# A bound on every gathered index in a graph network kernel

## The chip, the core and the metric

The kernel runs on one core of one Trainium2 chip. The metric is the time of one execution on the device, in microseconds (us). The median of three runs of the kernel before is 1931.74 us, with 1929.56 us as the lowest and 1933.11 us as the highest.

The engines are named as in the profile: PE is the matrix engine (PEld its weight loads), DVE, ACT and POOL are the vector, scalar and GpSimd engines, and SP is the engine that here only issues transfers. POOL is the one engine that issues an indirect DMA: a transfer that takes a list of row numbers from SBUF and fetches those rows of a table in HBM.

## The reference

There are 2,500 nodes with 256 features each, and 82,500 edges, sorted by their destination. Every edge has a source, a destination, a type from 0 to 7 and a weight. The first block is a relational graph convolution of two layers with a residual and a layer norm; the second is a network of three mean-aggregation layers with a residual and a layer norm.

```python
def _L0_gnn_ref(feat, norm, basis, coeff, bias, src, dst, etype):
    h = feat
    for l in range(2):
        W = jnp.einsum('rb,bio->rio', coeff[l], basis[l])
        all_h = jnp.einsum('ni,rio->rno', h, W)
        msg = all_h[etype, src] * norm
        agg = jax.ops.segment_sum(msg, dst, num_segments=2500)
        h = agg + bias[l]
        if l < 1:
            h = jax.nn.relu(h)
    return h

def _L1_gnn_ref(x, W_in, b_in, W_agg, W_self, b_hid, W_out, b_out, edge_index):
    dst, src = edge_index
    h = x @ W_in + b_in
    deg = jnp.maximum(jax.ops.segment_sum(ones, dst, 2500), 1.0)[:, None]
    for l in range(3):
        agg = jax.ops.segment_sum(h[src], dst, 2500) / deg
        h = jax.nn.relu(agg @ W_agg[l] + h @ W_self[l] + b_hid[l])
    return h @ W_out + b_out

x = _layernorm(x + _L0_gnn_ref(x, edge_weight1, ..., src, dst, edge_type_8))
x = _layernorm(x + _L1_gnn_ref(x, ..., stack([src, dst])))
```

## The kernel before

**Tiles of edges.** The edges are cut into T = 645 tiles of 128; the last tile holds 68. Each of the two layers of the first block (l = 0 and l = 1) goes through all tiles, so there are 1,290 tile visits, numbered n = l * 645 + t. In each visit the kernel needs the source row of each of the tile's edges: 128 rows of 1 KB, from the input `x` in layer 0 and from the DRAM table `H1`, the output of layer 0, in layer 1.

**Who fetches the rows.** In 14 of the visits (7 in each layer, ROW_TILES) SP fetches the rows one by one with plain transfers into `GS` (L1136). In the other 1,276 visits POOL fetches them, with one indirect DMA for a tile, issued by `rows_of` at L352 into one of NG = 16 slots of `G`. The row numbers are a column of `si`, or of `siF` for the first 15 tiles of layer 1. `G` is a part of the large tile `RY`, so the profile names such a gather `RY<-in_x,si`, `RY<-H,RX` or `RY<-H,si`.

**What orders the gathers.** `pool_setup` issues the first 16, and `pool_fast` the other 1,260 in order. Before each it waits on `s_sum` until PE has used the rows of the gather 16 places earlier, which frees the slot. Before layer 1 it waits for `H1` to be stored. After the last gather POOL converts eight blocks for the second part and does some of its output work.

**What uses the rows.** For every three tiles PE runs 12 matmuls at L1037 (`pe_sums_of`): the gathered rows are the weights, and a selection matrix that DVE makes from type, destination and edge weight (L631) is the moving operand. PE waits on `s_land[slot]` for the rows. DVE adds the sum to a window of accumulators (L623), and PE multiplies each finished window with the weights of the eight types (L885). Between these, in an order written out by hand, PE counts edges into an adjacency matrix (L867, L868) and, in layer 1, runs the first aggregation of the second block on windows that are done (L935). The second and third aggregation follow (L1281, L1247, L1291) and then the output (L1353); no gather is left by then.

A second program for inputs that don't fit this plan (`pool_general`) stands in the kernel too. It has indirect DMAs of its own, and isn't executed here.

Of the kernel before, what the change touches and what calls it, by code (L numbers as in the profile page):

```python
# [56 lines left out]
def edge_rows(t):  # L57
    return 128 if t < T - 1 else LASTP
# [110 lines left out]
def program(nc, x, ramp, ramp_col, src_rows, srcT, dstT, etT, wT, large, small, basis, coeff, bias, W_in, b_in, W_agg, W_self,  # L169
# [11 lines left out]
    with ExitStack() as ctx:  # L181
# [167 lines left out]
        def rows_of(e, n, table, index):  # L349
            t, slot = n % T, PLACE[n] % NG  # L350
            k = edge_rows(t)
            e.indirect_dma_start(G[0:k, slot, :], None, table, bass.IndirectOffsetOnAxis(ap=index[0:k, t:t + 1], axis=0)).then_inc(  # L352
                s_land[slot], 16)

        def pool_setup(e):
            e.wait_ge(s_src0, 16)
            for t in range(FIRST):
                rows_of(e, t, x, si)
# [75 lines left out]
        def pool_fast(e):  # L434
            e.wait_ge(s_src, 16)
            for p in range(FIRST, len(POOLED)):
                n = POOLED[p]
                e.wait_ge(s_sum, POOLED[p - NG] + 1)
                if n == T:
                    e.wait_ge(s_fixi, 4)  # L440
                    e.wait_ge(s_zrow, 32)
                    e.wait_ge(s_h1, 16 * (NW - 1))
                if n == T + FIX:
                    e.wait_ge(s_h1, 16 * NW)
                rows_of(e, n, x if n < T else H1, siF if T <= n < T + FIX else si)
            e.wait_ge(s_sum, 2 * T)
            e.wait_ge(s_dpe, NC * JB)
            e.wait_ge(s_ad, 16 * NA)
            for n in range(NR):
                e.wait_ge(s_ah[0], 16)  # L450
                e.tensor_copy(Ar[0:PB, n, :], Ah[0][:, n, :]).then_inc(s_arP, 1)
            for j in range(JB - 1):
                pool_bias(e, j)
            pool_norm(e, 16)
            pool_bias(e, JB - 1)
            pool_norm(e, 17)
            pool_norm(e, 18)
# [1470 lines left out]
```

## Time and profile before

| | |
|---|---|
| median of 3 runs | 1931.74 us (1929.56 to 1933.11) |
| span of the profiled execution, first to last instruction | 1935.5 us |
| PE busy | 1657.1 us (86%) |
| POOL busy | 1243.6 us (64%) |
| DVE busy | 1168.4 us (60%) |
| ACT busy | 487.5 us (25%) |
| mean busy share of the DMA engines, indirect gathers alone | 30.4% |
| mean granted TensorE clock | 0.963 of full speed |

The profile gives the profiled execution's time only as its span; it is 3.8 us (0.2%) above the median of the timed runs. An engine's busy time is the sum of its instructions. A line like `L352 POOL DMA_INDIRECT RY<-in_x,si x638` is one group of instructions: the line in the kernel, the engine, the operation, what it writes and reads, and how many there are. "idle before" is the time in which that engine stood still just before such an instruction, and the name after the arrow is what ended it; "issue" stands where nothing that the profile shows ended it. The share of busy time is an average over stages with different limits, so the stages are read one by one.

### The profile page before, as it was taken

The page shows a single profiled execution, that of the slowest core. Times are in us where ns is not written, and L with a number is a line of the kernel's source. Part 1 is how long each engine was busy: PE and PEld are TensorE (multiplying, and loading weights), DVE is VectorE, ACT ScalarE, POOL GpSimd, SP SyncE. Part 2 cuts the span into 40 slices and gives each one's busy share as a digit, 9 for nine tenths or more (in the row PEclk, how much of TensorE's full clock was granted, in tenths as well). Part 3 has the DMA queues.
Part 4 walks back from the last instruction along what each step waited for, and adds up shares of the span by engine and source line. Part 5 has one row for each costly group of instructions (what it writes and reads, how often), then busy time and mean ns, then how long its engine had stood idle before and what let it go on. Part 6 is the DMA issues. An engine that isn't in the chain of part 4 may idle for free.

```text
span 1935.5 us, 36034 instructions
## 1 busy us (share of the span) xinstructions
PE 1657.1 (86%) x9643; PEld 1378.2 (71%) x9643; DVE 1168.4 (60%) x4021; ACT 487.5 (25%) x1018; POOL 1243.6 (64%) x1311
## 2 busy tenths in 40 slices
PE   5787787887777778888899898888989999999997
PEld 3676666676566667676777787777777887777775
DVE  7978856656565656566777676775555563322344
ACT  2002111111211111122322222232455113433322
POOL 6777777777777777777777777777777773000011
PEclk9889999889999999999999999999999899999999
DMA  7344444444444444444444444445555442310011
GB/s 266 107 112 119 116 117 116 121 116 117 119 118 115 121 116 116 113 137 124 132 125 133 131 127 127 131 132 140 163 167 152 118 136 60 85 44 1 12 42 44
DMA packets 147633, 222.02 MB, mean 115 GB/s; under 512 B 81009, under 2 KB 103298, under 8 KB 147428
## 3 DMA queue, kind: packets, MB, share of 16 engines
q0 software_dynamic: 61344, 167.21, 30.4%
q1 hardware_dynamic: 49988, 38.78, 7.0%
q10 hardware_dynamic: 36096, 13.70, 2.6%
q8 instruction: 80, 1.31, 0.3%
q14 instruction: 125, 1.02, 0.2%
HBM read 202.31 MB, written 17.27 MB: 113 GB/s over the span
## 4 chain that ended last, share of the span: by engine, by line
PE 53%; DMA 31%; POOL 7%; issue 4%; DVE 3%; ACT 1%; DVEq 0%; ACTq 0%; POOLq 0%
PE bank L1037 21%; DMA RY<-in_x,si 19%; DMA RY<-H,si 12%; PE bank L1281 9%; PE bank L885 9%; POOL RY L352 7%; PE bank L935 3%; PE bank L1247 2%; PE bank L1291 2%; PE bank L868 1%; PE bank L1353 1%; PE bank L1002 1%; PE bank L852 1%; PE bank L950 1%; PE bank L908 1%
## 5 line engine op out<-in xcount | busy, mean ns | idle before, releaser
L1037 PE MATMUL bank<-RY 128*128 128x128 f32 x5104 | 768.9, 291 | 221.3 <-DMA RY<-in_x,si 146.8
L1037 PEld LDWEIGHTS bank<-RY 128*128 128x128 f32 x5104 | 678.9, 199 | 324.4 <-DMA RY<-in_x,si 187.7
L352 POOL DMA_INDIRECT RY<-in_x,si x638 | 611.2, 958 | 198.1 <-issue 136.9
L352 POOL DMA_INDIRECT RY<-H,si x623 | 595.0, 955 | 190.1 <-issue 138.4
L631 DVE TENSOR_SCALAR RY<-iot,c,wgt 128x128 f32<-128x128 f32 x1290 | 455.7, 358 | 389.3 <-PE bank L1037 388.2
L720 ACT CAST RY<-bank 128x320 uint8<-128x320 f32 x215 | 91.6, 426 | 684.2 <-PE bank L868 672.9
L509 DVE TENSOR_SCALAR RY<-iotN,bcol 128x320 bf16<-128x320 f16 x645 | 209.1, 324 | 0.0
L1281 PE MATMUL bank<-Ar,hs 125*128 125x500 f32 x800 | 203.9, 405 | 0.0
L623 DVE TENSOR_TENSOR RY<-RY,bank 128x256 f32 x430 | 178.4, 415 | 24.5 <-issue 13.0
L885 PE MATMUL bank<-RX,RY 128*128 128x256 f32 x704 | 189.1, 397 | 3.0 <-issue 1.8
L1342 POOL TENSOR_TENSOR x1b<-x1b,bo 125x256 f32<-125x256 f32 x20 | 14.8, 741 | 272.7 <-DMA x1b<-X 272.7
L885 PE MATMUL bank<-RY 128*128 128x256 f32 x704 | 184.3, 388 | 3.6 <-DVE RY L623 3.6
L868 PE MATMUL bank<-RY 128*128 128x320 bf16 x645 | 175.3, 310 | 0.5 <-DVE RY L509 0.5
L508 DVE TENSOR_SCALAR RY<-iotN,c 128x128 bf16<-128x128 f16 x645 | 175.2, 272 | 0.0
L1281 PEld LDWEIGHTS bank<-Ar,hs 125*128 125x128 f32 x800 | 150.6, 188 | 33.2 <-issue 4.6
L885 PEld LDWEIGHTS bank<-RY 128*128 128x128 f32 x704 | 129.5, 195 | 22.9 <-DVE RY L623 5.9
L885 PEld LDWEIGHTS bank<-RX,RY 128*128 128x128 f32 x704 | 130.8, 201 | 18.7 <-issue 2.0
L708 ACT COPY RY<-zero 128x576 f32<-128x576 f32 x176 | 109.5, 667 | 27.4 <-ACT RY L720 23.1
L935 PE MATMUL bank<-ArP,hsP 128*128 128x500 f32 x380 | 115.8, 425 | 0.4 <-DVE sagg L556 0.4
L777 ACT COPY RY<-bank 128x256 f32<-128x256 f32 x44 | 16.4, 373 | 314.6 <-PE bank L890 271.8
L556 DVE TENSOR_TENSOR sagg<-bank,sagg 128x500 f32<-128x500 f32 x90 | 60.6, 673 | 51.2 <-PE bank L935 51.1
L868 PEld LDWEIGHTS bank<-RY 128*128 128x128 bf16 x645 | 65.6, 102 | 27.1 <-issue 3.6
(148 smaller groups left out, 1311.3 us busy)
## 6 DMA issues: line engine op xcount, KB each, us to landing
ei<-in_x SPq DMA_DIRECT2D x896, 1.0 KB
ei<-H SPq DMA_DIRECT2D x896, 1.0 KB
RY<-in_x,si POOLq DMA_INDIRECT x638
RY<-H,si POOLq DMA_INDIRECT x623
Ad<-RY ACTq DMA_DIRECT2D x215, 40.0 KB
A<-Ad SPq DMA_DIRECT2D x22, 312.5 KB, 3.3
D<-Ad SPq DMA_DIRECT2D x20, 305.2 KB
RX<-in_basis ACTq DMA_DIRECT2D x2, 2048.0 KB, 21.7
```

Of the source, the lines that this page charges most:

```text
L352: e.indirect_dma_start(G[0:k, slot, :], None, table, bass.IndirectOffsetOnAxis(ap=index[0:k, t:t + 1], axis=0)).then_inc(s_land[slot], 16)
L508: e.tensor_scalar(Mr[:, u % NSL, :], iotN[:, 0:128], c1[:, u:u + 1], None, ALU.is_equal)
L509: e.tensor_scalar(Nr[:, u % NSL, :], iotN[:, :], bcol[:, u:u + 1], None, ALU.is_equal).then_inc(s_hot, 1)
L623: e.tensor_tensor(o, o, bank[2 + wg % 3][:, 0:256].rearrange("p (q c) -> p q c", c=16), ALU.add).then_inc(s_za, 1)
L631: e.tensor_scalar(S[:, v % NSS, :], iot[:, :], c2[:, u:u + 1], wgt[:, u:u + 1], ALU.is_equal, ALU.mult).then_inc(s_sel, 1)
L708: e.copy(o, zero[:, 0:1].to_broadcast([128, 4 * ZC])).then_inc(s_clear, 1)
L720: e.copy(Aw8[:, w % 4, :], bank[6 + w % 2][:, 0:NB]).then_inc(s_aw8, 1)
L868: e.matmul(b[:, 0:NB], Mr[0:k, a % NSL, :], Nr[0:k, a % NSL, :], start=(a == 0), stop=(i == TA - 1)).then_inc(s_cnt, 1)
L885: mm = e.matmul(bank[0][:, 0:256], ZA[:, s, q, 0:128], W[:, c, r * 256:(r + 1) * 256], start=(q == 0), stop=(g == 0 and q == 15))
L935: mm = e.matmul(unit_bank(q)[:, 0:CH], hsP[:, g % NP, part, mo * 128:(mo + 1) * 128], ArP[:, n % NV, :], start=(i + part == 0), stop=(i == ...
L1037: mm = e.matmul(bank[2 + wg % 3][:, c * 128:(c + 1) * 128], rows, S[0:k, n % NSS, :], start=(i == 0 and not ahead), stop=(i == TA - 1))
L1281: mm = e.matmul(bank[bs[mo]][:, 0:CH], hs[0:PB, j, q, mo * 128:(mo + 1) * 128], Ar[0:PB, n % NR, :], start=(j == 0 and q == 0), stop=(j == ...
```

## The change

The call of `indirect_dma_start` in `rows_of` gets two more arguments. `bounds_check` names the highest row number that counts as valid, here the table's last row: 2499 for `x`, and 2500 for `H1`, which has one row more. `oob_is_err=False` says that an index above the bound is no error: its row isn't copied, and nothing is reported. Without the two arguments, as before, no bound is named and the error mode is at its default, true. All indices in this input lie within the bound, so the same rows are moved. All 1,276 gathers are issued by this one call; the ones of `pool_general` go through another one and stay as they are.

```diff
         def rows_of(e, n, table, index):
             t, slot = n % T, PLACE[n] % NG
             k = edge_rows(t)
-            e.indirect_dma_start(G[0:k, slot, :], None, table, bass.IndirectOffsetOnAxis(ap=index[0:k, t:t + 1], axis=0)).then_inc(
+            e.indirect_dma_start(G[0:k, slot, :], None, table, bass.IndirectOffsetOnAxis(ap=index[0:k, t:t + 1], axis=0), bounds_check=table.shape[0] - 1, oob_is_err=False).then_inc(
                 s_land[slot], 16)
```

## Rows read from the trace of the kernel before

**Rows 1.** The page: busy time, and busy tenths in 40 slices.

```profile
PE 1657.1 (86%) x9643; PEld 1378.2 (71%) x9643; DVE 1168.4 (60%) x4021; ACT 487.5 (25%) x1018; POOL 1243.6 (64%) x1311
...
POOL 6777777777777777777777777777777773000011
```

**Rows 2.** The page: the chain of work that ended last, by engine.

```profile
PE 53%; DMA 31%; POOL 7%; issue 4%; DVE 3%; ACT 1%; DVEq 0%; ACTq 0%; POOLq 0%
```

**Rows 3.** Line L352 alone: durations in ns (min/median/max), first and last start.

```profile
L352 POOL DMA_INDIRECT RY<-in_x,si x638: 942/947/1682, 4.4 to 808.5; - x160
L352 POOL DMA_INDIRECT RY<-H,si x623: 942/947/1219, 830.3 to 1613.9; - x156
L352 POOL DMA_INDIRECT RY<-H,RX x15: 942/947/1009, 811.3 to 829.0; - x15
```

**Rows 4.** Timeline of POOL in layer 0: start us, duration us, instruction, idle before.

```profile
299.56 0.96 POOL L352 DMA_INDIRECT RY<-in_x,si  x1 [0.30 <-issue]
300.82 0.95 POOL L352 DMA_INDIRECT RY<-in_x,si  x1 [0.30 <-issue]
302.07 0.95 POOL L352 DMA_INDIRECT RY<-in_x,si  x1 [0.30 <-issue]
303.33 0.95 POOL L352 DMA_INDIRECT RY<-in_x,si  x1 [0.30 <-PE bank L1037]
```

**Rows 5.** Groups by line, PE's and POOL's: busy us, mean ns, idle before, releasers.

```profile
L1037 PE MATMUL bank<-RY 128*128 128x128 f32 x5104 | 768.9, 291 | 221.3 <-DMA RY<-in_x,si 146.8 <-DMA RY<-H,si 59.8 <-issue 7.0
...
L352 POOL DMA_INDIRECT RY<-in_x,si x638 | 611.2, 958 | 198.1 <-issue 136.9 <-PE bank L1037 57.3 <-DMA si<-in_srcT 4.0
L352 POOL DMA_INDIRECT RY<-H,si x623 | 595.0, 955 | 190.1 <-issue 138.4 <-PE bank L1037 51.6
```

**Rows 6.** Busy time by stage: window and length, then PE, PEld, DVE, ACT, POOL.

```profile
400.00:600.00 200.00, 156.34 (x972) 128.80 (x971) 119.45 (x473) 33.58 (x71) 151.53 (x160) 0.97 0.42 117
...
1090.00:1350.00 260.00, 229.58 (x1456) 196.66 (x1455) 178.63 (x661) 74.46 (x161) 197.19 (x207) 0.97 0.47 131
1350.00:1500.00 150.00, 138.24 (x881) 114.20 (x880) 77.25 (x221) 79.80 (x161) 113.73 (x120) 1.00 0.58 160
1500.00:1614.00 114.00, 110.40 (x645) 94.33 (x644) 67.97 (x182) 24.71 (x53) 86.15 (x92) 0.94 0.45 126
```

**Rows 7.** Timeline of POOL where layer 0 ends, its last tile (68 rows) at 808.54.

```profile
807.29 0.95 POOL L352 DMA_INDIRECT RY<-in_x,si  x1 [0.30 <-PE bank L1037]
808.54 1.22 POOL L352 DMA_INDIRECT RY<-in_x,si  x1 [0.30 <-issue]
811.34 0.96 POOL L352 DMA_INDIRECT RY<-H,RX  x1 [1.57 <-DMA H<-RY]
```

**Rows 8.** Timeline of POOL where layer 1 ends, its last tile at 1613.93.

```profile
1612.68 0.95 POOL L352 DMA_INDIRECT RY<-H,si  x1 [0.30 <-issue]
1613.93 1.10 POOL L352 DMA_INDIRECT RY<-H,si  x1 [0.30 <-PE bank L1037]
1624.47 4.45 POOL L451 CAST Ar<-AhG 125x500 fp32r<-125x500 uint8 x8 [9.43 <-PE bank L1037]
```

**Rows 9.** Timeline of POOL at the start of the program.

```profile
0.25 0.10 POOL L1921 MEMSET const-float32-0.0<- 128x1 f32 x1 [0.25 <-issue]
0.28 0.10 POOL L1921 MEMSET const-float32-1.0<- 128x1 f32 x1
0.31 0.10 POOL L1921 MEMSET const-bfloat16-1.0<- 128x1 bf16 x1
...
4.43 1.16 POOL L352 DMA_INDIRECT RY<-in_x,si  x1 [4.00 <-DMA si<-in_srcT]
```

**Rows 10.** Timeline of PE where layer 1 ends: its last work on gathered rows.

```profile
1620.20 1.50 PE L1037 MATMUL bank<-RY 128*128 128x128 f32 x12
1621.46 1.60 PE L974 MATMUL bank<-ArP,hsP 128*128 128x500 f32 x6
1622.90 1.50 PE L1037 MATMUL bank<-RY 128*128 128x128 f32 x12
```

## The prediction

> **What bounds the kernel now.** I read the page first. PE is busy 86% of the span and POOL only 64%, but POOL's slices stand at an unbroken 7, from the second slice to the 32nd, and fall to nearly 0 after that [rows 1]. A share that never moves for 1,600 us is either an engine waiting in a steady rhythm or one that never waits at all. The chain of work that ended last puts 31% of the span on landing DMAs and 7% on POOL, beside 53% on PE [rows 2]. So a good part of the end is set by gathers, and the question is what paces them: the slot that has to come free, the transfer, or POOL's own time for issuing one.
>
> The timeline of POOL answers it. A gather starts every 1.25 us: 0.95 us busy and 0.30 us idle [rows 4]. The idle time is 0.30 us when "issue" ended it, and 0.30 us when a wait for PE's sums is named too, so that wait had long been met. The whole groups say the same: 388 us of idle before 1,276 gathers is 0.30 us for each [rows 5]. The gathers run from 4.43 us to 1613.93 + 1.10 = 1615.03 us [rows 8, 9], and 1610.6 us / 1,276 is 1.262 us. POOL is therefore saturated from the first gather to the last; the missing tenths in the page are a gap that belongs to each gather. The times are also strikingly even: 942 ns at least, 947 ns as the median, in all three groups and with whatever row numbers [rows 3].
>
> PE on its side waits for gathered rows: 146.8 us in layer 0 and 59.8 us in layer 1, in its matmul groups [rows 5]. In the stages, PE is busy 156 of 200 us in the middle of layer 0 and 230 of 260 us in the middle of layer 1, but 248.6 of 264 us from 1350 us to the end of the gathers [rows 6]. So POOL sets the pace up to about 1350 us (638 gathers of layer 0 and some 430 of layer 1), and for the last 208 or so both run at about the same pace, with PE a little behind. Between the last gather's end at 1615.0 us and PE's last matmuls on gathered rows at 1622.9 us lie 7.9 us [rows 8, 10]; a gather of 3 to 4 us in flight leaves some 4 us of slack at that point.
>
> **What the change does, part by part.** No instruction is added to PE, DVE, ACT or SP, no wait is added or removed, no buffer or order moves, and the same rows in the same transfers are fetched, since no index lies above the bound. What can change is what POOL does for each of 1,276 gathers. Anything it does is on the path: a microsecond on POOL before 1350 us is a microsecond at the end, since nothing there covers it. Behind a late gather stand the next gathers on POOL's own queue; 3 tiles' sums on PE wait for it, then DVE's add to the window, and the whole rest of the layer.
>
> The trace has no gather with a bound, so each part is priced from both sides by the nearest rows.
>
> (a) Handing the bound to the gather. At least nothing: it can travel in the instruction, or be set once for each of the two tables. At most one more small instruction on POOL for each gather. The four memsets at the start begin 0.03 us apart [rows 9], and I take that as the price of one more small instruction in POOL's stream. The ends are 0 and 0.03 us, and I take the middle, 0.015 us. By the Trainium skill ("Advanced Engine Details and Errata", Engine Queue Depths) GpSimd has a queue of 8 entries, so its sequencer may run ahead of the work and such an instruction would be hidden: by that rule this part is 0 instead of 1,276 x 0.015 = 19 us. That the gap of 0.30 us doesn't grow when a wait is named [rows 4] agrees with it, though it doesn't prove it.
>
> (b) Comparing 128 row numbers with the bound, and being ready to leave rows out. It falls into the busy part, 947 ns for 128 rows, or 7.4 ns a row if all of it went by rows. At least nothing: the comparison can be there already, against a bound that never bites; the nearest row is the distance from the minimum to the median, 5 ns [rows 3]. At most what an unusual gather costs here: the two of 68 rows take 1.22 and 1.10 us [rows 7, 8] against 0.947 us for 128 rows. Fewer rows take longer, so POOL has a quick way for the full tile and another for the rest, and the other is up to 0.27 us longer. Between 0.005 and 0.27 us, a factor of 54 apart, I take the geometric middle, 0.037 us; it is about 4% of the busy part, which is what one more test among the steps that make a row's transfer would be.
>
> (c) Dropping the error mode. It removes work only if some is done now, when no bound is named that an index could break. I take 0, and keep a gain as a rival.
>
> The sum is 0.015 + 0.037 = 0.052 us a gather, and 1,276 x 0.052 = 66 us. Off it goes the slack at the end of layer 1, about 4 us, because the last 208 gathers come 208 x 0.052 = 11 us later to a PE that is that much behind. PE's later stages, from 1623 us on, hang on no gather. So the span goes from 1935.5 to about 1997.5 us, +62 us, and the median of the runs, which stands 3.8 us lower, from 1931.7 to 1993.7 us; I forecast 1993 us. With the two upper ends together it is 1,276 x 0.30 = 383 us, 2,310 us; with both lower ends nothing.
>
> **The rivals.**
>
> *Nothing changes* (chance 0.34). The comparison is always made, or hides inside the 947 ns, and the bound costs no instruction. For it: the duration doesn't depend on the index values, which is how it would look if the work were done over many rows at once, where one comparison more is a few ns. Under 3 ns a gather it is 1,276 x 0.003 = 4 us, 0.2% of the time, and that is about what a measurement of this kernel can tell from no change. Time: 1928 to 1936 us.
>
> *Faster* (0.17). Place: the end of each gather at L352, where an error would be reported. If the default mode costs a check there, the new mode drops it. A price in the size of the one small instruction, 0.03 us, would reach the end wherever PE waits for rows: (638 + 430) x 0.03 = 32 us, 1900 us; the last 208 gain nothing, since PE has no idle time left to give. It decides as soon as what it saves exceeds (a) and (b) together, 0.052 us if those are real and 0.003 us if they are not. Its limit is PE's 206.6 us of waiting for gathers [rows 5], 1725 us. Against it: nothing in the trace shows such a check, and no bound is named before that could be broken.
>
> *The full tile loses its quick way* (0.05). If the bound sends every gather through a way that treats row by row, the 68-row gather prices it: 1.10 us / 68 x 128 = 2.07 us, 1.12 us more than 0.947, and 1,276 x 1.12 = 1,430 us gives 3,360 us. It decides if any step has to branch for each row. The Trainium skill ("GPSIMD Engine Reference", section 3.1) says that data-dependent branching costs about 12 cycles an element, at 1.2 GHz (its section 1): an estimate by that page is 128 x 12 / 1.2 = 1,280 ns a gather, 1,633 us in all, 3,565 us. The page speaks of elements of a kernel's loop, and a rarely taken branch need not cost that; against the rule stands that now a whole row costs at most 7.4 ns, 9 cycles of that clock, with every step of it.
>
> **How the numbers follow.** The forecast's mechanism, POOL longer by 0.003 to 0.30 us a gather, gets 0.44; with the lost quick way slower holds 0.49, nothing 0.34, faster 0.17. The likeliest one's own range goes from 0.01 us a gather (+12 us, 1944 us) to 0.235 us (+300 us, 2230 us). The range for the time has to take in "nothing" as well, and the smaller gains: from 1905 us, which is a gain of 0.025 us on 1,068 gathers, to 2230 us. Outside are the larger gains (about 0.10), the lost quick way (0.05) and the last part of the mechanism (0.04).
>
> **What the profile of the changed kernel would show.** The first place is line L352 alone: its median against 947 ns is (b), and its idle before against 0.30 us is (a). The period of POOL times 1,276 must give the end of the last gather, now 1615 us. If POOL is longer, PE's idle time behind `DMA RY<-in_x,si` grows by nearly 638 times the difference, and behind `DMA RY<-H,si` by less than that; PE's busy time stays. If the two 68-row gathers no longer stand out from the others, the way has changed. The stretch after the last gather should stay as long as now, about 320 us, in every case.
>
> **What would make it wrong.** A comparison that is already made or that costs single ns; a default error mode that has a price; or a price per row that is far over 4% of the present time. The direction rests on POOL having no cover; the size rests on (b), which no row of the trace shows.

## The result, and the profile after

The changed kernel takes 2000.77 us as the median of 4 runs (1998.78 to 2003.65), and the kernel before 1931.83 us in runs beside it (4 runs, 1929.56 to 1933.11). The ratio is 1.0354, with a 95% interval of 1.0341 to 1.0367: 69 us slower. The forecast was 1993 us and 62 us slower.

Line L352 alone, in the kernel after (durations in ns as minimum/median/maximum, then first and last start in us), beside [rows 3]:

```profile
L352 POOLq MOVE  x1276: 29/29/38, 4.0 to 1668.0; - x183
L352 POOL DMA_INDIRECT RY<-in_x,si x638: 994/998/1842, 4.9 to 844.2; - x160
L352 POOL DMA_INDIRECT RY<-H,si x623: 994/998/1273, 865.9 to 1682.8; - x156
L352 POOL DMA_INDIRECT RY<-H,RX x15: 994/999/1223, 845.9 to 864.6; - x15
```

Two things are new. Each gather's median went from 947 to 998 ns, nearly alike in all three groups, and the minimum rose as much (from 942 to 994 ns). So every gather pays it, and it is no wait. And there is one MOVE of 29 ns for each gather on POOLq, POOL's own instruction queue; that it puts the bound into a register is borne out by the kernel with one register below. The timeline of POOL in layer 0 shows that it isn't seen between the gathers, whose idle time is 0.30 us as in [rows 4]:

```profile
299.62 1.02 POOL L352 DMA_INDIRECT RY<-in_x,si  x1 [0.30 <-issue]
300.94 1.00 POOL L352 DMA_INDIRECT RY<-in_x,si  x1 [0.30 <-issue]
302.24 0.99 POOL L352 DMA_INDIRECT RY<-in_x,si  x1 [0.30 <-issue]
303.54 1.00 POOL L352 DMA_INDIRECT RY<-in_x,si  x1 [0.30 <-issue]
```

The groups by line (busy us, mean ns, idle before and what ended it), beside [rows 5]:

```profile
L1037 PE MATMUL bank<-RY 128*128 128x128 f32 x5104 | 787.9, 294 | 266.8 <-DMA RY<-in_x,si 166.6 <-DMA RY<-H,si 83.4 <-issue 8.3
...
L352 POOL DMA_INDIRECT RY<-in_x,si x638 | 646.1, 1013 | 198.8 <-issue 142.7 <-PE bank L1037 51.6 <-DMA si<-in_srcT 4.5
L352 POOL DMA_INDIRECT RY<-H,si x623 | 628.2, 1008 | 190.1 <-issue 143.7 <-PE bank L1037 46.4
```

The page's sums, beside [rows 1]:

```profile
PE 1677.5 (84%) x9643; PEld 1389.0 (70%) x9643; DVE 1164.9 (58%) x4021; ACT 487.5 (24%) x1018; POOL 1313.1 (66%) x1311
```

POOL is busy 1313.1 - 1243.6 = 69.5 us longer, and the kernel takes 69 us longer. The idle time before the gathers is the same to a microsecond (198.8 and 190.1 us, against 198.1 and 190.1 us). PE's share of the change is split: it waits 43 us longer for gathered rows (250.0 against 206.6 us), and is busy 20 us longer, at a mean granted clock of 0.958 against 0.963. The last gather of each layer on POOL's timeline, beside [rows 7] and [rows 8]:

```profile
844.17 1.17 POOL L352 DMA_INDIRECT RY<-in_x,si  x1 [0.30 <-issue]
845.88 1.02 POOL L352 DMA_INDIRECT RY<-H,RX  x1 [0.55 <-issue]
...
1682.77 1.16 POOL L352 DMA_INDIRECT RY<-H,si  x1 [0.31 <-issue]
1687.60 4.43 POOL L451 CAST Ar<-AhG 125x500 fp32r<-125x500 uint8 x8 [3.66 <-PE bank L1037]
```

The last one ends at 1683.9 us, 68.9 us after that of the kernel before. Both layers have their part: layer 1's first gather, which waits for `H1` to be stored, starts at 845.88 in place of 811.34 us, 34.5 us later, and the rest is added after it. From the last gather to the end of the span it is 314.5 us, 6 us less than before (320.5 us). PE's timeline shows what became of the slack at the end of layer 1:

```profile
1685.06 0.73 PE L1037 MATMUL bank<-RY 128*128 128x128 f32 x4
1686.36 1.16 PE L1037 MATMUL bank<-RY 68*128 68x128 f32 x8 [0.57 <-DMA RY<-H,si]
```

PE now waits 0.57 us for the last gather itself, and starts on its rows 2.4 us after POOL is done with it. In the kernel before PE's last matmuls ran without a wait, 7.9 us after it [rows 10]. How much of the 6 us is the change's is taken up with the slack, further down.

### The profile page after: what moved, and what is told of

Same layout as the page of the kernel before. It is cut to its first block, busy times and chain, and to the rows that moved or that the text cites. A ratio compares the mean times of both kernels' runs of the same rounds, so it can differ in the third digit from the quotient of the medians.

```text
span 1998.4 us, 37310 instructions
## 1 busy us (share of the span) xinstructions
PE 1677.5 (84%) x9643; PEld 1389.0 (70%) x9643; DVE 1164.9 (58%) x4021; ACT 487.5 (24%) x1018; POOL 1313.1 (66%) x1311
## 3 DMA queue, kind: packets, MB, share of 16 engines
q0 software_dynamic: 61344, 167.21, 29.5%
## 4 chain that ended last, share of the span: by engine, by line
PE 46%; DMA 32%; issue 10%; POOL 9%; DVE 2%; ACT 1%; POOLq 0%; DVEq 0%; ACTq 0%
PE bank L1037 19%; DMA RY<-in_x,si 18%; DMA RY<-H,si 13%; PE bank L1281 9%; POOL RY L352 9%; PE bank L885 6%; PE bank L935 2%; PE bank L1247 2%; PE bank L1291 2%; PE bank L868 1%; PE bank L1353 1%; PE bank L852 1%; PE bank L908 1%; PE bank L1002 1%; PE bank L950 1%
## 5 line engine op out<-in xcount | busy, mean ns | idle before, releaser
L1037 PE MATMUL bank<-RY 128*128 128x128 f32 x5104 | 787.9, 294 | 266.8 <-DMA RY<-in_x,si 166.6
L1037 PEld LDWEIGHTS bank<-RY 128*128 128x128 f32 x5104 | 688.8, 201 | 379.8 <-DMA RY<-in_x,si 215.4
L352 POOL DMA_INDIRECT RY<-in_x,si x638 | 646.1, 1013 | 198.8 <-issue 142.7
L352 POOL DMA_INDIRECT RY<-H,si x623 | 628.2, 1008 | 190.1 <-issue 143.7
L631 DVE TENSOR_SCALAR RY<-iot,c,wgt 128x128 f32<-128x128 f32 x1290 | 460.9, 362 | 445.0 <-PE bank L1037 441.3
L509 DVE TENSOR_SCALAR RY<-iotN,bcol 128x320 bf16<-128x320 f16 x645 | 198.3, 307 | 0.0
L885 PE MATMUL bank<-RX,RY 128*128 128x256 f32 x704 | 184.9, 391 | 2.8 <-issue 1.9
L868 PE MATMUL bank<-RY 128*128 128x320 bf16 x645 | 178.1, 314 | 0.2
L935 PE MATMUL bank<-ArP,hsP 128*128 128x500 f32 x380 | 121.1, 441 | 0.4 <-DVE sagg L556 0.4
L868 PEld LDWEIGHTS bank<-RY 128*128 128x128 bf16 x645 | 66.0, 102 | 27.2 <-issue 3.1
```

Of the source, the lines that this page charges most:

```text
L509: e.tensor_scalar(Nr[:, u % NSL, :], iotN[:, :], bcol[:, u:u + 1], None, ALU.is_equal).then_inc(s_hot, 1)
L631: e.tensor_scalar(S[:, v % NSS, :], iot[:, :], c2[:, u:u + 1], wgt[:, u:u + 1], ALU.is_equal, ALU.mult).then_inc(s_sel, 1)
L868: e.matmul(b[:, 0:NB], Mr[0:k, a % NSL, :], Nr[0:k, a % NSL, :], start=(a == 0), stop=(i == TA - 1)).then_inc(s_cnt, 1)
L885: mm = e.matmul(bank[0][:, 0:256], ZA[:, s, q, 0:128], W[:, c, r * 256:(r + 1) * 256], start=(q == 0), stop=(g == 0 and q == 15))
L935: mm = e.matmul(unit_bank(q)[:, 0:CH], hsP[:, g % NP, part, mo * 128:(mo + 1) * 128], ArP[:, n % NV, :], start=(i + part == 0), stop=(i == ...
L1037: mm = e.matmul(bank[2 + wg % 3][:, c * 128:(c + 1) * 128], rows, S[0:k, n % NSS, :], start=(i == 0 and not ahead), stop=(i == TA - 1))
```

## Experiments

Every ratio below is against the kernel before on the same chip. The first four ran where the kernel before takes 1933 us, the next four where it takes 2275 us, and the last four where it takes 2296 us. What that means for them stands with the fifth.

### Which part of the change costs

**The bound alone, an index over it being an error.**

```diff
-            e.indirect_dma_start(..., axis=0)).then_inc(
+            e.indirect_dma_start(..., axis=0), bounds_check=table.shape[0] - 1).then_inc(
```

> The bound alone, with the error mode left at its default. Theory (the test of the row numbers costs): the median gather stays at 998 ns, idle before it at 0.30 us, the time within 0.3% of the changed kernel, about 2000 us. Rival (leaving rows out silently is what costs, by a way that must be ready to drop a row): with an index over the bound as an error the gather goes back towards 947 ns and the time to about 1932 us.

Measured: 2019.48 us, ratio 1.0445 (1.0428 to 1.0463), which is 86 us slower than before and some 18 us slower than the changed kernel. Line L352 alone:

```profile
L352 POOLq MOVE  x1276: 29/29/35, 4.1 to 1688.1; - x183
L352 POOL DMA_INDIRECT RY<-in_x,si x638: 1007/1012/1552, 5.0 to 854.4; - x160
L352 POOL DMA_INDIRECT RY<-H,si x623: 1007/1012/1229, 877.3 to 1701.3; - x156
```

The bound is what costs, and neither theory had the rest right: with the bound named, treating an index over it as an error costs another 14 ns (1012 against 998), and dropping the error mode saves that.

**The mode alone.**

```diff
-            e.indirect_dma_start(..., axis=0)).then_inc(
+            e.indirect_dma_start(..., axis=0), oob_is_err=False).then_inc(
```

> oob_is_err=False alone, no bound named. Theory: no index is tested, the median gather stays at 947 ns, no register instruction appears on POOL's queue, the time is within 0.2% of 1932 us. Rival (the mode costs): 998 ns and about 2000 us. Second rival (the default mode costs something, which the changed kernel's bound hides): under 947 ns, and faster by up to 1,276 times the difference, 13 us for each 10 ns.

Measured: 1931.83 us, ratio 0.9994 (0.9985 to 1.0004). Line L352 alone:

```profile
L352 POOL DMA_INDIRECT RY<-in_x,si x638: 942/946/1682, 4.2 to 807.8; - x160
L352 POOL DMA_INDIRECT RY<-H,si x623: 942/946/1212, 829.5 to 1611.5; - x156
```

Nothing changes. So the default mode costs nothing as long as no bound is named, and the "faster" rival has nothing to gain.

**The register set once for each table.**

```diff
+        def set_limit(e, rows):
+            if not limit:
+                limit.append(e.alloc_register("limit"))
+            e.reg_mov(limit[0], rows - 1)
...
-            e.indirect_dma_start(..., axis=0)).then_inc(
+            e.indirect_dma_start(..., axis=0), bounds_check=limit[0], oob_is_err=False).then_inc(
```

`set_limit` is called ahead of the first gather and again ahead of layer 1.

> The changed kernel with the bound in a register that is set once for each table, in place of one MOVE of 29 ns for each gather. Theory (the MOVE is hidden, the gather's own 51 ns are the cost): gather 998 ns, period 1.30 us, about 2000 us, no gain. Rival (the MOVE is part of the 51 ns or of the gap): the period is up to 0.03 us shorter, and the time up to 1,276 x 0.029 = 37 us less, 1964 us.

Measured: 2002.63 us, ratio 1.0354 (1.0336 to 1.0372), the same ratio as the changed kernel. The gathers stand at L359 here:

```profile
L354 POOLq MOVE  x2: 35/36/38, 0.7 to 830.4; - x2
L359 POOL DMA_INDIRECT RY<-in_x,si x638: 994/998/1847, 4.2 to 845.1; - x160
L359 POOL DMA_INDIRECT RY<-H,si x623: 994/998/1263, 866.5 to 1683.4; - x156
```

With 2 MOVEs in place of 1,276 the gathers keep their 998 ns and the kernel its time. The MOVE is hidden, and all of the cost lies inside the gather.

**Eight idle MOVEs ahead of each gather, no bound.**

```diff
         def rows_of(e, n, table, index):
...
+            for _ in range(8):
+                e.reg_mov(spare[0], table.shape[0] - 1)
```

> The kernel before with eight idle MOVEs into a register ahead of each gather and no bound: 8 x 29 = 232 ns of instructions on POOL's queue for each gather. Theory (POOL's queue runs ahead of the engine and has over 1 us for each gather): gather 947 ns, idle before 0.30 us, time within 0.2% of 1932 us. Rival (the queue's work is in the 0.30 us between two gathers): the gap grows by 0.2 us and the time by 1,276 x 0.23 = 296 us.

Measured: 1933.38 us, ratio 0.9996 (0.9986 to 1.0006). This tells nothing: the profile counts 36,034 instructions, as many as for the kernel before, and none of the MOVEs is among them, so they never ran, probably because nothing reads that register. How much room POOL's queue has beyond one MOVE stays open.

### What the step inside the gather does

**64 rows of each tile, without and with the bound.**

```diff
-            k = edge_rows(t)
+            k = min(64, edge_rows(t))
...
-                    n, k = l * T + t - TA + 1 + i, edge_rows(t - TA + 1 + i)
+                    n, k = l * T + t - TA + 1 + i, min(64, edge_rows(t - TA + 1 + i))
...
-                        rows = GS[:, q % 2, c * 128:(c + 1) * 128]
+                        rows = GS[0:k, q % 2, c * 128:(c + 1) * 128]
```

> The kernel before with only the first 64 rows of every tile gathered and summed; half of the edges' messages are left out, every instruction else stays. Theory (the 947 ns of a full gather go largely by rows, so a test made for each row can weigh 51 ns): well under 947 ns, 600 to 750 ns; the kernel then runs at PE's own pace, at least 1932 - 206.6 = 1725 us. Rival (the time is a fixed part, or the full tile has a quick way that 64 rows lose, as the 68-row gathers at 1.10 and 1.22 us suggest): 900 ns or more, and about 1930 us or slower.

> The same with the bound named and no error for an index over it. Theory (the 51 ns are a test for each row, 0.4 ns a row): 25 ns over the 64-row gather without a bound. Rival (a fixed step, paid once for each gather, such as reading the register and setting up a second limit): 51 ns over it.

Measured: 2327.3 us without the bound (ratio 1.0135, 1.0114 to 1.0157) and 2370.95 us with it (1.031, 1.0283 to 1.0338). What counts here is the gather's own duration. First without and then with the bound:

```profile
L352 POOL DMA_INDIRECT RY<-in_x,si x638: 897/903/1692, 4.2 to 966.2; - x160
```

```profile
L352 POOL DMA_INDIRECT RY<-in_x,si x638: 937/942/1554, 5.0 to 990.1; - x160
```

| median ns | 64 rows | 128 rows | for each row | rest |
|---|---|---|---|---|
| no bound | 903 | 947 | 0.69 | 859 |
| bound | 942 | 998 | 0.88 | 886 |
| difference | 39 | 51 | 0.19 | 27 |

The last two columns are the straight line through the two sizes; that other sizes lie on it isn't shown. By this line a gather is some 860 ns of fixed work and 0.7 ns a row, not 7.4 ns a row, and the bound adds about 27 ns once and 0.19 ns for each row: both theories hold half of it. "Well under 947 ns" for 64 rows didn't come true, and nor did a penalty for the smaller tile; the rival was right in that nearly all of the time is a fixed part.

These runs also say something on the two 68-row gathers of [rows 7, 8]. In the kernel with 64 rows and no bound the last gather of each layer stands at the same place, but fetches 64 rows:

```profile
966.15 0.90 POOL L352 DMA_INDIRECT RY<-in_x,si  x1 [0.30 <-issue]
1994.19 0.90 POOL L352 DMA_INDIRECT RY<-H,si  x1 [0.30 <-issue]
```

They take 0.90 us like all others. So it isn't the place that makes a 68-row gather slow (1.10 to 1.22 us), nor that the tile is small: 64 and 128 rows are quick, and 68 rows don't lie on the line above. Why this count is slow, and which other counts are, wasn't tried.

**A bound that bites.** The slots of G are zeroed once by POOL, ahead of the first gather.

```diff
-            e.indirect_dma_start(..., axis=0)).then_inc(
+            e.indirect_dma_start(..., axis=0), bounds_check=table.shape[0] // 2, oob_is_err=False).then_inc(
...
+            e.memset(G, 0.0).then_inc(s_gz, 1)
```

> The bound is set to row 1250, so that half of the rows are left out; the slots of G are zeroed first, and left-out rows keep what their slot held, so part of the sums is missing. Theory (the test is one step for a row that costs the same whichever way it falls): gather 998 ns as in the changed kernel, software queue packets about halved, time about 2000 us, less what shorter transfers save in flight. Rival (dropping a row is a branch that costs when taken): a longer gather, by up to 64 times the price of one; at 10 ns each 0.64 us, and 1,276 x 0.64 = 817 us more. Second rival (a dropped row saves the writing of its transfer): a gather under 998 ns.

Measured: 2311.95 us, ratio 1.0173 (1.0131 to 1.0216), 37 us slower. This time can't be set beside a kernel that bounds all gathers and drops nothing, since none ran on that chip; it also holds 3.5 us for zeroing G. What counts is the gather's own duration. The gathers at L353:

```profile
L353 POOL DMA_INDIRECT RY<-in_x,si x638: 995/1002/1837, 5.2 to 971.8; - x160
```

And the page's line of the software queue, which carries the gathers (packets, MB, share of the DMA engines):

```profile
q0 software_dynamic: 61344, 83.78, 13.5%
```

Half of the bytes are gone (83.78 against 167.21 MB in the kernels that move all rows), in the same number of packets (61,344), which were expected to be halved, and the gather is 4 ns longer than with a bound that leaves nothing out. If those 4 ns belong to the some 64 rows that are dropped, dropping one costs 0.06 ns. A branch for each dropped row, or a saving for each, would show far more.

### Where the added time reaches the end

**The bound in layer 0 only, and in the last 208 visits only.**

```diff
+            how = dict(bounds_check=table.shape[0] - 1, oob_is_err=False) if n < T else {}
-            e.indirect_dma_start(..., axis=0)).then_inc(
+            e.indirect_dma_start(..., axis=0), **how).then_inc(
```

For the other the condition is `n >= 2 * T - 208`; 206 gathers fall under it, since SP fetches two of those tiles.

> The bound named in layer 0 only, 638 gathers. Theory (each gather of layer 0 is on the path with nothing to cover it): 638 x 0.051 = 33 us more than before, 1965 us; the gathers of layer 1 stay at 947 ns. Rival (the cost is given back in layer 1, whose PE has its own limit): well under 30 us.

> The bound named in the last 208 visits only, from about 1350 us on, where PE is busy 94% of the time. Theory (PE is a little behind the gathers there and hides part of it): 208 x 0.051 = 10.6 us later on POOL, of which 4 us are hidden: +6.6 us, 1939 us. Rival one (all of it reaches the end): +10.6 us, 1943 us. Rival two (PE sets the pace there): within 2 us of before.

Measured: 2290.55 us for layer 0 (ratio 1.0071, 1.0045 to 1.0097), 15.8 us over the 2274.8 us of the kernel before on that chip, and 2277.86 us for the last 208 visits (1.0013, 1.0000 to 1.0027), 3.1 us over it. The gathers themselves are as expected, 998 ns with the bound and 946 ns without, but they don't set the pace on this chip. The groups of the layer 0 kernel:

```profile
L1038 PE MATMUL bank<-RY 128*128 128x128 f32 x5104 | 786.9, 306 | 114.0 <-issue 108.4 <-DVE RY L632 3.7 <-DMA RY<-in_x,si 1.1
...
L869 PE MATMUL bank<-RY 128*128 128x320 bf16 x645 | 196.3, 331 | 105.3 <-DVE RY L510 63.8 <-issue 32.5 <-DVE RY L632 8.1
...
L353 POOL DMA_INDIRECT RY<-in_x,si x638 | 646.0, 1013 | 324.5 <-issue 164.7 <-remote 84.3 <-PE bank L1038 71.1
L353 POOL DMA_INDIRECT RY<-H,si x623 | 595.0, 955 | 365.6 <-issue 140.9 <-remote 125.1 <-PE bank L1038 99.6
```

POOL is idle 690 us before them, in place of 388 us. Within a layer the program lets a gather wait for nothing but a slot that PE has to free, so the some 300 us on top are put down to that; the profile itself names PE for a part of them and gives "remote", a releaser that it can't identify, for another. PE in turn stands still 108.4 us before its matmuls on gathered rows for nothing that the profile shows ("issue"), and 1.1 us for the gathers of layer 0, in place of 146.8 us in [rows 5]. It also waits 63.8 us for DVE's tiles before it counts edges (L869), a wait of 0.5 us where the kernel before takes 1932 us. Of the 35 us by which the gathers of layer 0 are longer in sum (646.0 against 611.2 us), 45% reach the end; the rest falls into POOL's waits. Both were run again:

> The bound in layer 0 only, run once more, because on the chip of the first run PE's own stalls and not the gathers set the pace. Where the kernel before takes 1932 us, theory (nothing covers a gather of layer 0): 638 x 0.051 = 33 us more, 1965 us. Rival (given back in layer 1): well under 30 us. On a chip where the kernel before takes 2275 us: about 16 us more, as in the first run.

> The bound in the last 208 visits only, run once more for the same reason. Where the kernel before takes 1932 us, theory (4 us of 10.6 hidden by PE being behind): +6.6 us, 1939 us. Rival one (all of it reaches the end): +10.6 us. Rival two (PE sets the pace there): within 2 us of before.

The third chip is of the same kind, at 2295.7 us for the kernel before. Layer 0 alone gives 2318.0 us, 22.3 us more (ratio 1.0094, 1.0072 to 1.0117), and the last 208 visits give 2301.12 us, 5.4 us more (1.0023, 1.0008 to 1.0037). That is 64% of 35 us, and half of 206 x 0.052 = 10.7 us. The intervals are wide: 6 us to either side for layer 0, 3 us for the last 208 visits. The theories on cover speak of a chip where the gathers set the pace, so these four experiments don't decide them. For such a chip the changed kernel itself shows that all of layer 0's added time is there when layer 1 starts (34.5 of 34.9 us); whether an unbounded layer 1 would give some back stays open.

**More tiles fetched by SP.**

```diff
-ROW_TILES = [96 + 84 * j for j in range(7)]
+ROW_TILES = [96 + 52 * j for j in range(10)]
```

> The kernel before, no bound, with ten tiles of each layer fetched row by row by SP in place of seven, 52 tiles apart in place of 84: POOL issues 1,270 gathers, 6 fewer. Theory (POOL's gathers set the pace): 6 x 1.25 = 7.5 us less, 1925 us. Rival (SP, which needs some 0.44 us for a row, so 57 us for a tile against 65 us between two, comes late): slower than before.

Measured: 2412.06 us, ratio 1.0605 (1.0574 to 1.0636), on the chip where the kernel before takes 2274.8 us. The waits of PE (us in total, times, longest us) show why; `ei` is the tile that holds the rows fetched by SP:

```profile
PE bank L1037 <- DMA ei<-in_x: 127.0, 9, 15.6
PE bank L1037 <- issue: 121.0, 151, 4.9
...
PE bank L1037 <- DMA ei<-H: 38.6, 5, 11.7
```

The rival won there: the row-by-row tiles come too late, in 14 of 20 cases, by up to 15.6 us, and the 165.6 us of waiting are more than the 137 us that the kernel lost. Whether it would help where the gathers set the pace stays open.

## Why the prediction was right, point by point

**POOL sets the pace and has no cover.** Right where the kernel before takes 1932 us, and shown by three kernels there; on the slower chips the gathers don't set the pace. The time of a kernel follows the summed duration of its gathers one for one:

| kernel | gathers' busy us, summed | over before | time over before, us |
|---|---|---|---|
| before | 1220.6 | | |
| changed | 1289.8 | 69 | 69 |
| one register | 1291.3 | 71 | 70 |
| bound as error | 1307.5 | 87 | 86 |

No wait was added, no engine became the bound, and PE's longer waits are the consequence. That PE waits 20 us longer in layer 0 and 24 us longer in layer 1, and not "nearly 638 times the difference", 33 us, in layer 0, is a miss, and so is "less than that" for layer 1. The rest is in PE's own busy time, which was said to stay and grew by 20 us. The mean granted clock fell a little (0.963 to 0.958); by itself it would make 1657.1 us into 1665.7 us, 9 of the 20 us, so the larger part of this growth has no cause shown.

**(a) Handing over the bound: priced 0.015 us, measured 0.** The instruction is there, and costs 29 ns, as long as the 0.03 us that was read from the memsets' starts; but the kernel with one register shows that it is hidden. The Trainium skill's rule ("Advanced Engine Details and Errata", Engine Queue Depths: 8 entries for GpSimd, so the queue can run ahead) gave 0, and the runs agree with it for one instruction. They say nothing on the depth.

**(b) Comparing the rows: priced 0.037 us, measured 0.051 us.** The price was 0.014 us too low, and the two ends (0.005 and 0.27 us) held the measured value. The reasoning behind it was weaker than the number. It took up to 7.4 ns a row where the runs with 64 rows give 0.69 ns, and the upper end was the price of the 68-row gathers, which says nothing on a full tile. The middle of two ends so far apart could as well have missed by a factor of several. The mean gather grew by 0.054 us, a little more than the median, and 1,276 x 0.054 = 69 us.

**(c) Dropping the error mode: priced 0, measured 0 without a bound.** With a bound it is a gain of 14 ns a gather, about 18 us in all, which the change takes in already.

**The sum.** 0.052 us a gather was forecast and 0.051 us measured, which is luck in part: (a) was 0.015 us too high and (b) 0.014 us too low, and the two misses cancel. The direction and the place, POOL's own time without cover, were earned; that the size came out within 8 us wasn't.

**The slack of 4 us.** No row ahead of the prediction shows the "3 to 4 us in flight" that it is worked out from; in the changed kernel PE starts on the last gather's rows 2.4 us after that gather's end, 3.6 us after its start. The slack is real, but the 6 us above overstate it, because the profiled execution of the kernel before was a long one: its span is 3.8 us above the median of the timed runs, and that of the changed kernel 2.4 us below. The time from the last gather's end to POOL's next instruction, a CAST that waits for PE's sums, is 9.4 us in the kernel before, 5.7 us with the mode alone and 8.4 us with the idle MOVEs; it is 3.7, 5.5 and 4.3 us in the changed kernel, with one register and with the bound as error. The means differ by 3.3 us, near the 4 us of the prediction. The medians (69 us, against 69.5 us more on POOL) show none of it, at an uncertainty of some 2.5 us; PE's longer busy time can have taken it back, which isn't shown. The prediction also says both that this slack goes and that the stretch after the last gather stays as long as now, and the two don't agree.

**The rivals.** "Nothing changes" fell with the 51 ns. "Faster" fell with the mode alone. The lost quick way fell too: the median gather of a full tile is 0.95 to 1.01 us in every kernel, and the two 68-row gathers still stand out (1.17 and 1.16 us against 0.998 us). The Trainium skill's 12 cycles for each element with data-dependent branching ("GPSIMD Engine Reference", section 3.1) would, as an estimate, be 1,280 ns a gather; the bound costs 51 ns, and with half of the rows dropped 55 ns, so nothing of that size is paid here. The rival's own price came from a wrong reading of the 68-row gathers: a gather of 64 rows takes 903 ns, so the 1.10 us can't be shared out by rows.

## What to carry to other kernels

When one engine repeats an instruction some thousand times with nothing to cover it, an option of that instruction is a term of the sum: here 54 ns in the mean, times 1,276, are 69 us, 3.5% of the kernel. Read first whether the idle time between two of them is the same whatever is waited for; if so, that engine can be saturated at 64% busy, as here. Name a bound on a gather only where an index can be out of range, and if one is named, leaving the row out costs 14 ns less a gather than reporting an error. Fill the gather as far as it goes, since 128 rows cost 5% more than 64, and time any other count before using it, since 68 rows cost more than 128.

## What the runs showed that was not expected

**A gather's time is nearly all fixed.** It takes 903 ns for 64 rows and 947 ns for 128 rows of 1 KB, but 1.10 to 1.22 us for 68 rows.

**The same kernel takes 1932, 2275 or 2296 us in three groups of runs, each on another chip.** The gathers last 946 to 947 ns in all three. The mean granted clock is 0.88 to 0.90 in the slower two, against 0.96 to 0.97. There the queues themselves stand still at times: the register MOVEs that SP issues for its single rows have the same median of 29 ns, but reach 1.4 us. The row of the kernel before is given first, where it takes 1932 us, and then those of the kernel with the last 208 visits bounded:

```profile
L1136 SPq MOVE ei<-in_x x896: 29/29/38, 47.8 to 729.1; - x180
```

```profile
L1137 SPq MOVE ei<-in_x x896: 2/29/1401, 51.6 to 883.1; - x180
L1137 SPq MOVE ei<-H x896: 2/29/1383, 992.2 to 1869.4; - x180
```

PE's idle time put down to "issue" grows along with it (7.0 us in [rows 5], 108.4 us above). PE is also busy some 100 us longer (1754 to 1774 against 1657 us), which leaves the larger part of the 340 us to waiting. What holds up the queues wasn't tested, nor whether it goes with the chip or with the hour. It matters for reading such a result: the change costs 3.5% where the gathers set the pace, and on the slower chips 29 to 64% of the added time reached the end, by the medians of the four experiments with a part of the gathers bounded.

**With half of the rows PE takes longer.** In the kernel with 64 rows and no bound PE is busy 1999.2 us, against 1773.5 us in the kernel with the last 208 visits bounded on the same chip, and the mean granted clock is 0.823 against 0.891. The number of its matmuls and the shape of their outputs are the same. The ratio of the two clocks alone would make 1773.5 us into 1920 us, some 147 of the 226 us that PE is busy longer. Matmuls that read no gathered rows are slower too: those that count edges (L868) take 359 ns in the mean, against 335 ns. The kernel is 1.4% slower, although its gathers are shorter. Why the clock was granted lower isn't shown; by design the two kernels differ in the rows that the matmuls at L1037 use, and with them in the bytes that are fetched. The stretch from 400 to 600 us in both (length, then PE, PEld, DVE, ACT, POOL busy, granted clock), first with all rows, then with 64:

```profile
400.00:600.00 200.00, 142.51 (x799) 119.27 (x799) 97.73 (x394) 28.45 (x60) 125.46 (x133) 0.85 0.35 98
```

```profile
400.00:600.00 200.00, 171.47 (x821) 130.72 (x820) 95.69 (x395) 27.96 (x59) 119.65 (x132) 0.76 0.21 55
```
